# A fused graph and expert layer on one core: order of work in the last block of layer 1

## The reference, cut to what matters

```python
def _block(x, edge_index, edge_weight, g, bln, W, b):          # twice: W6, then W7
    h = _layer_norm(x, g, bln)
    h = _gcn_conv(h, edge_index, edge_weight, W, b)            # segment_sum((h @ W.T)[row] * norm, col) + b
    return x + relu(h)

gnn = _block(_block(xn, ..., W6, b6), ..., W7, b7) @ Wp.T + bp
msg = _layernorm(attention(xn) @ Wm, g1, b1)
mix = xn + _layernorm(relu(concatenate([xn, msg]) @ W1) @ W2, g2, b2)
x = x + gnn + mix
x = x + ffn(_layernorm(x))                                     # top 2 of 8 experts
```

## Time and profile before

| what | before |
|---|---|
| median of 3 runs | 4481.67 us |
| profiled execution, own time | 4480.88 us |
| its span | 4479.2 us |
| TensorE matmuls busy | 3663.7 us (82%) |
| TensorE weight loads busy | 3083.7 us (69%) |
| VectorE busy | 2481.9 us (55%) |
| GpSimd busy | 3180.8 us (71%) |
| ScalarE busy | 1227.8 us (27%) |
| mean granted TensorE clock | 0.916 |

### The profile page before, as it was taken

How to read it: one execution, slowest core, us unless ns; L and a number is a source line. 1 busy time by engine, 2 the same in 40 slices (tenths; PEclk the granted TensorE clock), 3 DMA queues, 4 the chain that set the end, 5 groups by cost and what they waited for, 6 DMA issues and landing times.

```text
span 4479.2 us, 94972 instructions
## 1 busy us (share of the span) xinstructions
PE 3663.7 (82%) x27016; PEld 3083.7 (69%) x27017; DVE 2481.9 (55%) x8820; ACT 1227.8 (27%) x3172; POOL 3180.8 (71%) x3542
## 2 busy tenths in 40 slices
PE   4876777676776777777768999999999999999998
PEld 3765655565565555555656888887788887888877
DVE  7544554455555555544545565665566565665555
ACT  1330100110010101001013444444444444444444
POOL 4457777777777777777767777777777777777772
PEclk8998888888888888888889999999999999999999
DMA  4034444444444444444433343343344343343331
GB/s 142 29 107 118 130 130 119 129 130 120 126 129 126 128 124 125 130 119 129 126 107 112 108 116 114 112 116 114 108 116 116 109 116 114 111 117 113 116 106 42
DMA packets 256029, 515.37 MB, mean 115 GB/s; under 512 B 61464, under 2 KB 154016, under 8 KB 255968
## 3 DMA queue, kind: packets, MB, share of 16 engines
q0 software_dynamic: 151392, 413.60, 32.4%
q1 hardware_dynamic: 104576, 101.17, 6.9%
HBM read 474.81 MB, written 39.71 MB: 115 GB/s over the span
## 4 chain that ended last, share of the span: by engine, by line
PE 41%; DVE 17%; POOL 12%; issue 11%; DMA 7%; DVEq 2%; ACT 2%; POOLq 0%; SPq 0%; ACTq 0%
PE bank L1198 40%; POOL gs L548 12%; DMA gr<-h_d,idx_r 6%; DVE ss L965 5%; DVE rstd L729 2%; DVE rstd L728 1%; DVE rstd L730 1%; PE bank L1221 1%; DVE st L737 1%; DVEq L965 1%; DVE w L1096 1%; DVE u L746 1%; DVE mv L741 1%; DMA out<-u 1%; DVEq L256 1%
## 5 line engine op out<-in xcount | busy, mean ns | idle before, releaser
L548 POOL DMA_INDIRECT gs<-h_d,idx_all x3038 | 2934.6, 966 | 951.3 <-issue 694.6
L1198 PE MATMUL bank<-gs,ss 128*128 128x256 f32 x6272 | 1594.0, 401 | 13.7 <-DMA gs<-h_d,idx_all 12.6
L1198 PEld LDWEIGHTS bank<-gs,ss 128*128 128x128 f32 x6272 | 1214.4, 201 | 192.6 <-DMA gs<-h_d,idx_all 22.5
L965 DVE TENSOR_SCALAR ss<-iw,dst_f,ew 128x128 f32<-128x128 f32 x3152 | 888.7, 361 | 116.6 <-PE bank L1198 64.8
L1198 PE MATMUL bank<-experts,w 128*128 128x256 f16 x4896 | 622.3, 281 | 26.8 <-DVE w L1096 26.8
L1198 PE MATMUL bank<-w,experts 128*128 128x128 f16 x9792 | 614.4, 219 | 1.2 <-DVE w L1102 1.2
L1198 PEld LDWEIGHTS bank<-w,experts 128*128 128x128 f16 x9792 | 570.4, 98 | 50.2 <-issue 16.6
L1198 PEld LDWEIGHTS bank<-experts,w 128*128 128x128 f16 x4896 | 478.8, 101 | 108.0 <-DVE w L1096 36.0
L1198 PE MATMUL bank<-gr,sr 128*128 128x256 f32 x232 | 116.9, 599 | 456.1 <-DMA gr<-h_d,idx_r 456.1
L1198 PEld LDWEIGHTS bank<-gr,sr 128*128 128x128 f32 x232 | 48.9, 260 | 503.3 <-DMA gr<-h_d,idx_r 503.0
L709 ACT ACTIVATE hT<-bank,eb1c 128x128 f32<-128x128 f32 x816 | 232.6, 368 | 448.0 <-PE bank L1198 437.1
(11 more groups left out here) (263 smaller groups left out, 3912.9 us busy)
## 6 DMA issues: line engine op xcount, KB each, us to landing
gs<-h_d,idx_all POOLq DMA_INDIRECT x3038, 2.7
hself<-h_d SPq DMA_DIRECT2D x100, 128.0 KB
ew_in<-in_eW SPq DMA_DIRECT2D x49, 168.0 KB
out<-u SPq DMA_DIRECT2D x51, 128.0 KB
u<-xn_d SPq DMA_DIRECT2D x50, 128.0 KB
h_d<-u SPq DMA_DIRECT2D x50, 128.0 KB, 1.8
u<-x_d SPq DMA_DIRECT2D x50, 128.0 KB
u<-r_d SPq DMA_DIRECT2D x50, 128.0 KB
```

The lines of the kernel that those rows point to most:

```text
L548: pool.indirect_dma_start(gs[:, n, :], None, table[:, :], bass.IndirectOffsetOnAxis(ap=idx_all[:, w, n:n + 1], axis=0)).then_inc(s[f"main_ ...
L965: m = dve.tensor_scalar(ss[:, slot + j, :], iw[:, :], dst_f[:, bass.ds(c, 1)], ew[:, bass.ds(c, 1)], ALU.is_equal, ALU.mult)
L1198: return pe.matmul(out_ap, lhsT, rhs, start=first, stop=last, **kw)
```

## The change

In TensorE's program the last block of layer 1 is written out behind the loop of the 48 others. In it, group 7 of the messages and the leftovers stand directly behind group 6, ahead of the `w1` products; the flip of `xn` and the `w2` products follow. In VectorE's program the last block norms the row first, signals it, and only then waits for the `w2` product and norms that, in a second chain (14 more links, which layer 2's chain counts are told of). In every block, `next_h` now issues the bias product after the wait for bank 7 and ahead of the wait for `zT`. SyncE, ScalarE and GpSimd are as they were.

```diff
-                dve.wait_ge(s["y1_ps"], w + 1)
-                z_ins, y_ins = layer_norm(dve, tc, (u5[:, :], u3[:, :]), (wide(4), t_c[1][:, :]))
-                z_ins.then_inc(s["z1_done"], 1)
+                if last:
+                    z_ins, = layer_norm(dve, tc, (u5[:, :], u3[:, :]))
+                    z_ins.then_inc(s["z1_done"], 1)
+                    dve.wait_ge(s["y1_ps"], w + 1)
+                    y_ins, = layer_norm(dve, tc, (wide(4), t_c[1][:, :]))
+                else:
+                    dve.wait_ge(s["y1_ps"], w + 1)
+                    z_ins, y_ins = layer_norm(dve, tc, (u5[:, :], u3[:, :]), (wide(4), t_c[1][:, :]))
+                    z_ins.then_inc(s["z1_done"], 1)
...
-                tc = Chain(dve, s["dve_links"], ch.n + W * L1_LINKS, LN_LINKS + 5, w)
+                tc = Chain(dve, s["dve_links"], ch.n + W * L1_LINKS + LN_LINKS, LN_LINKS + 5, w)
...
             def next_h(w):
+                pe.wait_ge(s["h2_done"], w)
+                mm(wide(7), ones_row[:, :], hb[:, 1, :], True, False)
                 pe.wait_ge(s["z1T_set"], w + 1)
-                pe.wait_ge(s["h2_done"], w)
-                by_rows(7, zT, w7, s["h7_ps"], bias=hb[:, 1, :])
+                for k in range(KB):
+                    m = mm(wide(7), zT[:, k, :], w7[:, k, :], False, k == KB - 1)
+                m.then_inc(s["h7_ps"], 1)
...
-            with pe.Fori(0, W) as w:
+            def window1(w, last=False):
...
                 for k in range(PIECES):
-                    messages(w, v, k)
+                    if not (last and k == PIECES - 1):
+                        messages(w, v, k)
+                    if last and k == 6:
+                        messages(w, v, PIECES - 1)
+                        rest_messages(*rest_table(pe, 0, w))
...
-                        n_rest, base = rest_table(pe, 0, w)
+                        if not last:
+                            n_rest, base = rest_table(pe, 0, w)
...
-                rest_messages(n_rest, base)
+                if not last:
+                    rest_messages(n_rest, base)
+
+            with pe.Fori(0, W - 1) as w:
+                window1(w)
+            window1(W - 1, last=True)
```

More of the change, by code:

```diff
@@ L1067, in window1 @@
                 dve.tensor_tensor(u6[:, :], t_c[1][:, :], t_c[0][:, :], ALU.add).then_inc(s["r_done"], 1)
-                assert tc.n == tc.per, tc.n
+                assert tc.n == tc.per + (LN_LINKS if last else 0), tc.n
             with dve.Fori(0, W - 1) as w:
```

## The result

The changed kernel takes 4496.16 us (median of six runs, 4491.89 to 4502.57), the kernel before 4480.52 in its six runs. The ratio is 1.0034, 95% interval 1.0024 to 1.0044: 15.6 us slower where 2.6 us faster were forecast. The profiled execution took 4492.21, near the lowest of the six (span 4490.5 against 4479.2, 11.3 more); it is these 11.3 us that the trace can show.

A forecast was written before the change was run, and what follows sets the result against it. The seam between the layers was taken as the bound, with layer 2 hanging on its first gather: 2344.77 to 2342.2, a gain of 2.6, so 4480.88 became 4478.3, and 4479.1 with 0.79 for the median; range 4476.0 to 4482.8.

The forecast's parts named there:

- I carry the shift through in full: Layer 2: the first gather's shift at the seam, 2.6 us earlier, was taken to reach the program's end undiminished.
- Part 3: Seam, VectorE: row normed alone, its flip 3.2 earlier; the mix's norm then waits for w2 and needs 3.21.
- part 6: Last block written out outside TensorE's loop: taken as 0, with bounds of 0 and 0.3 lost.
- Rows 2: Trace rows of layer 2: gathers wait 343.3 us on only their own issue, TensorE 116.1 us on leftover gathers.
- The gathers as a fixed 1.25 pace: Last block of layer 1: gathers go out every 1.25 (0.94 and 0.30 of issue) and set the messages' time.
- Part 1: Last block, TensorE: leftover product 2.76 after its gather's issue, acc read 3.77 earlier; register loads taken as 0.
- Part 2: Last block, TensorE: w1, relu and w2 behind the leftovers; w1 groups take 3.6, w2 ends at 2334.85.
- the clock rival: Seam: TensorE at 1.2 GHz through w1 and w2, 3.3 us slower, 4485.0; half of w1 low leaves 0.8 gain; chance 0.08.
- Parts 3, 4 and 5: Seam: norms in series, bias product hidden by the zT copy, r_d write gating h2_d's by 0.60; gain 2.6.
- one in layer 2 that at worst took the gain back: Layer 2: the seam's shift exists but the end does not move, 4481.7; chance 0.13.

The follow-up runs named there:

- e2_pe_part: TensorE's part of the change alone, VectorE's program as in the kernel before: 4483.38 us, ratio 1.0006.
- e5_before_psum: The kernel before, with gelu writing back into its PSUM bank so that `hidden_low` has one SBUF input instead of two: 4449.25 us, ratio 0.9931.
- e8_seam_psum: e6_after_psum with the last h2_d write ahead of r_d's and waited for alone, and leftover lookups ahead of the last messages: 4444.72 us, ratio 0.9918.
- e4_after_wait: The changed kernel with 2 empty semaphore increments behind the four lookups in each block of layer 2: 4481.46 us, ratio 0.9999.
- e6_after_psum: The changed kernel with the gelu edit of e5_before_psum: 4447.28 us, ratio 0.9927.
- e3_before_14: The kernel before with 14 empty semaphore increments in VectorE's program between the layers: 4496.29 us, ratio 1.0035.
- e7_before_psum_14: e5_before_psum with the 14 increments between the layers of e3_before_14: 4448.08 us, ratio 0.9927.

## Why the prediction was wrong

- *"I carry the shift through in full"* is the step that failed. It took layer 2 as fixed, because no line of it changed and its waits are on gathers. The runs showed that layer 2 starts 0.5 earlier (2344.28 against 2344.77) and then runs 0.25 us a block slower, because the added VectorE instructions moved a pause of 0.12 in its loop, and gathers then started behind `hidden_low` and were held by it. Part 3 counted the second norm's instructions as time in the seam, never as code in front of a loop; part 6 asked that question for TensorE only, where it did not matter (e2_pe_part).
- *The gathers as a fixed 1.25 pace.* Rows 2 gave the gather stream as nearly the pace of layer 2, which was right: any change of it goes to the end. But I read the 0.94 row of the timeline as its price. The profile's page of the kernel before has a mean of 966 ns over both layers, and layer 2 alone has 980 (the line under e5_before_psum) against 946 undisturbed, 49 us over 1524 gathers. Some 36 of the 49 stand beside `hidden_low`. Asking what made up those 34 ns would have shown both the risk and the larger gain.
- *Part 1* was mis-sized by 0.8: the leftover product started 3.54 after its gather's issue, not 2.76. The register lookups, for which the bounds were 0 and 0.30, stand in front of it. With the lookups ahead of the last messages (e8_seam_psum) it started 2.78 after, so they are the term.
- *Part 2 and the clock.* w1 took 5.4 (first product 2328.42, relu released at 2333.82) instead of 3.8. The granted clock had been 1.00, with TensorE busy for 1.56 of 4.00; it then fell to 0.50 (1.2 GHz) from 2328.6 to 2332.0, in w1:

```profile
2324.00:2328.00 4.00, 1.56 (x6) 0.71 (x6) 2.00 (x7) 0.00 (x0) 0.99 (x2) 1.00 0.26 72
2328.00:2332.00 4.00, 4.00 (x20) 3.94 (x21) 3.06 (x13) 0.00 (x0) 0.00 (x0) 0.58 0.10 35
```

  This is the mild half of the clock rival (a half of w1 low, 1.8, a gain of 0.8 left); it cost 1.6 and with the 0.8 of part 1 leaves about the measured 0.3. In e4_after_wait and e6_after_psum the same order had full clock through w1 (3.82 and 3.77), and seams of 18.25 and 18.47 against the forecast 17.7: at the clock that was assumed, only the term of part 1 is off. In both, as in the kernel before, a stretch at the low clock ended within 0.25 of the leftover's issue. So at like clock the new order gave 1.8 to 2.0 of the forecast 2.6, and the 0.3 of the one pair is in part the luck of the clock.

  With TensorE's old order the seam varies too: 20.0 to 20.3 in four traces, and 18.6 in the three (e3_before_14, e5_before_psum, e7_before_psum_14) in which the full clock held throughout from before the leftover's issue. By the rule of the Trainium skill, "TensorE: Matmul & The Clock Gate", section "What's actually happening", that activity releases the throttled clock, the sparser order was exposed. The clock fell in w1 in two of the five traces with that order (the changed kernel and e2_pe_part).
- *Parts 3, 4 and 5* were right: the norms in a row, the bias hidden (1.14 between bias and W7 product became 0.63), no gain of it in the loop, and the r_d write as the gate, to 0.54 where 0.60 was taken.
- The rivals had a slower case of 3.3 us at the seam, and one in layer 2 that at worst took the gain back. None made layer 2 itself slower, so the range (to 4482.8) missed by 13 us.

## What to carry to other kernels

When GpSimd's gathers set the pace, price them by the mean of the group against the shortest one, and ask what VectorE does in the difference: here a VectorE instruction with two SBUF inputs that started just ahead of a gather held it until its own end. Where one input can come from PSUM, try that before tuning the place, since a place that is good by 0.1 us can be lost by an edit elsewhere. And an edit that adds instructions ahead of a loop can change that loop; the control is the same number of empty instructions.

## What the runs showed of the hardware that was not expected

- A pause of 0.12 us recurs at one place of VectorE's looped instruction stream and moves with the number of instructions in front of the loop: one for one with 3, 14 and 28 added. What it is stays open. The Trainium skill, "Advanced Engine Details and Errata", section "ISA Cache", gives instruction lines of 256 instructions; a crossing of such a line would look like this, and no run here shows that it is one.
- A gather that finds `hidden_low`, with two SBUF inputs, running for 0.05 or more takes until 0.82 after the end of it; one that starts up to 0.02 behind it still takes 0.94 to 0.96. With one input in PSUM none is held.
- Two table lookups on TensorE ahead of the leftover product put its start 3.35 to 3.72 behind the gather's issue in the changed order (four traces), against 2.78 with the lookups moved (e8_seam_psum). The prediction had put them at 0.
